# A deformable-convolution stage whose sampling window is six rows high instead of eight, with a separate stage for the samples that reach further

## The reference, cut to what matters

```
xr   = conv1x1(gn(x), w_reduce)            # 192 -> 180 channels
offs = conv1x1(xr, w_offset)               # 360 channels
off_w, off_h = offs[:, :180], offs[:, 180:]
# deform_conv2d, for each of 10 groups of 18 channels and each of 9 taps (ky, kx):
sy = off_y + (ky - 1) + h ;  sx = off_x + (kx - 1) + w
val = bilinear sample of xr at (sy, sx), zero outside the image
f_w, f_h = einsum('bikhw,oik->bohw', val, weight)     # 1620 x 180, one for each of two convolutions
attn = softmax(conv1x1(mean(f_w + f_h), w_attn))      # per image
out  = conv1x1(attn0 * f_h + attn1 * f_w, w_expand)
```

## Time and profile before

| | us |
|---|---|
| median of 3 runs | 13394.25 (13377.7 to 13395.6) |
| profiled execution, first to last instruction | 13389.0 |
| projections, from the first matmul of a chunk to the flag | about 82 to 474 |
| sampling and convolution, first DMA to last store | 474.9 to 8550 |
| all later stages | 8553 to 13389 |

### The profile page before, as it was taken

One profiled execution on the slowest core, in us unless ns is written; L12 is line 12 of the kernel. 1 busy time (PEld: TensorE's weight loads), 2 busy tenths in 40 slices (PEclk: granted clock), 3 DMA queues, 4 the chain that ended last, 5 costly groups with the idle time before them and its releaser, 6 DMA issues. The chain is left out here.

```text
span 13389.0 us, 237451 instructions
## 1 busy us (share of the span) xinstructions
PE 12626.2 (94%) x81086; PEld 10422.1 (78%) x81086; DVE 11629.7 (87%) x15744; ACT 11084.4 (83%) x13077; POOL 6971.2 (52%) x3614
## 2 busy tenths in 40 slices
PE   7899999999999999999999999988089989999999
PEld 4799999999999999999999999743053345555555
DVE  4699999999999999999999999778987878888888
ACT  2588888888888888888888888539777889899898
POOL 0255555555555555555555555303320068888887
PEclk9999999999999999999999999779599999999999
...
GB/s 122 162 178 177 178 178 178 178 178 178 178 178 178 178 177 178 178 178 177 177 178 178 177 178 178 189 149 153 136 173 143 156 111 104 99 106 104 100 104 85
DMA packets 824757, 2102.23 MB, mean 157 GB/s; under 512 B 83236, under 2 KB 430810, under 8 KB 681562
## 3 DMA queue, kind: packets, MB, share of 16 engines
...
## 5 line engine op out<-in xcount | busy, mean ns | idle before, releaser
L518 PE MATMUL dc_p<-dc_t 96*128 96x144 f32 x51948 | 6846.0, 285 | 21.1 <-PEq L515 20.8
L585 POOL TENSOR_TENSOR dc_t<-dc_t 128x648 f32<-128x648 f32 x2885 | 4526.4, 1569 | 4021.9 <-POOLq L584 3977.9
L518 PEld LDWEIGHTS dc_p<-dc_t 96*128 96x128 f32 x51948 | 6529.5, 189 | 42.4 <-issue 21.5
L645 DVE TENSOR_TENSOR dc_t<-dc_p,dc_t 128x1296 f32<-128x1296 f32 x2886 | 4342.9, 1505 | 507.3 <-DVEq L643 444.5
L464 ACT ACTIVATE dc_t<-dc_t 96x1152 f32<-96x1152 f32 x2892 | 3590.1, 1241 | 463.6 <-ACTq L488 462.3
L466 ACT ACTIVATE dc_t<-dc_t 96x1152 f32<-96x1152 f32 x2892 | 3367.8, 1165 | 347.5 <-ACTq L465 10.4
L2161 DVE TENSOR_TENSOR_SCAN ms_t<-ms_t,ms_p 128x512 f32<-128x512 f32 x1728 | 2127.7, 1271 | 282.8 <-PE ms_p L2103 204.6
L2077 POOL TENSOR_TENSOR ms_t<-ms_t 128x1536 f32<-128x1536 f32 x576 | 1987.8, 3456 | 503.5 <-DVE ms_t L2161 499.7
L2113 PE MATMUL ms_p<-ms_t,top_t 128*128 128x512 f32 x3456 | 1774.7, 596 | 0.0
L559 PE MATMUL dc_p<-dc_t 128*128 128x180 f32 (+1 forms) x7488 | 1633.5, 318 | 17.0 <-PEq L554 10.9
L2103 PEld LDWEIGHTS ms_p<-top_t,ms_t 128*128 128x128 f32 x6912 | 849.7, 141 | 967.6 <-issue 693.8
...
## 6 DMA issues: line engine op xcount, KB each, us to landing
dc_t<-sxd SPq DMA_DIRECT2D x1446, 864.0 KB, 5.7
ms_t<-bcd SPq DMA_DIRECT2D x576, 256.0 KB, 3.3
...
```

The costliest lines, as they stand in the source:

```text
L518: ins = e.matmul(PT[j % 2][:, t // 3, (t % 3) * 144:(t % 3 + 1) * 144], HX[:, m // 2 % RP, m % 2, t * 128:(t + 1) * 128], XW[:, i, ky:ky + ...
L585: e.tensor_tensor(z[:, :, 0:HALF], z[:, :, 0:HALF], z[:, :, HALF:2 * HALF], ALU.add)\
L645: e.tensor_tensor(Zt[:, n % 4, :].rearrange("p (b m i) -> p b m i", b=3, i=CG), PT[n % 2][:, :, 0:432].rearrange("p b (m i) -> p b m i", i ...
```

## The change

1. The sampling window is 6 rows instead of 8 (`WIN`), so the moving operand of a sample matmul is 108 columns instead of 144, `weigh` takes 972 columns instead of 1296, `halve` 486 instead of 648 (now into a tile of its own, `ZH`). Three rows remain: `quarter` adds the first two of them, `sum_rows` the third (324 columns each). `NWIN` is 17 instead of 13.
2. A window of 6 rows holds only samples whose vertical offset lies within `REACH` = 2.5 rows of its centre. In the projections stage the two reductions are replaced by the eight largest distances per partition and their indices (`max`, `max_index`), of an absolute value that ScalarE makes (`size`); SyncE also fills a DRAM array `cor` with zeros (96 DMAs of 270 KB).
3. A new stage `far_samples` collects up to 128 samples beyond reach, gathers their coordinates, the four `xr` vectors and the convolution weights by indirect DMAs from GpSimd, computes their contribution to the output, writes it to `cor` with an indirect DMA, and initialises `SUM` with it. It writes the flag: the loop over all windows is taken if there are more than 128 such samples, or more than 7 in a partition.
4. In sampling, each tile loads its part of `cor` and a factor (`kept_loads`), and GpSimd (`keep`) multiplies `ACC` by the factor and adds the correction, twice 128 x 360 once in a tile; VectorE's `scalar_tensor_tensor` in `add_up` becomes a `tensor_tensor`.
5. ScalarE makes hats for two steps in one instruction, 96 x 2304, and issues the Abs of the next pair ahead of the Relu of this one.
6. The tile store is issued by SyncE, in the row of its loads, instead of by ScalarE, one tile later than before.

```
-WIN = 8
-NWIN = 13
+WIN = 6
+NWIN = 17
-FAR = 3.0
+REACH = 2.5
+NCAND = 8
...
+                    for i in (2 * c, 2 * c + 1):
+                        e.dma_start(k.cor_z[i], Z[:, :, :].rearrange("p r c -> p (r c)")).then_inc(s_zs, 16)
...
+                    for u in range(3):
+                        ins = e.activation(AB[:, c % 3, u * CM:(u + 1) * CM], OY[:, c % 2, u, :], ACT.Abs,
+                                           bias=DT[:, u:u + 1])
...
+                def largest(c):
+                    e.wait_ge(s_ab, c + 1)
+                    e.max(k.CV[:, c, :], AB[:, c % 3, :]).then_inc(s_v, 1)
+                    e.wait_ge(s_v, 1).then_inc(s_v, -1)
+                    e.max_index(k.CI[:, c, :], k.CV[:, c, :], AB[:, c % 3, :]).then_inc(s_mx, 1)
...
-                    e.tensor_reduce(MM[:, 0, c:c + 1], OY[:, q, :, :], AX.XY, ALU.max)
-                    e.tensor_reduce(MM[:, 1, c:c + 1], OY[:, q, :, :], AX.XY, ALU.min).then_inc(s_o2, 1)
...
+                def kept_loads(i, b, ti, y):
+                    e.dma_start(CR[:, i, :], k.cor_v[DS(b * NT + y, 1)].rearrange("a p c -> (a p) c")).then_inc(s_cr[i % 2], 16)
+                    e.dma_start(KF[:, i:i + 1],
+                                k.d["c_keep"][DS(ti, 1)].rearrange("a p c -> (a p) c")).then_inc(s_cr[i % 2], 16)
...
+                            if q == 3:
+                                done = b * NT + y if i >= 2 else e.snap(((w + 15) >> 4) * NRB + (b * NT + y))
+                                store_tile(i, done, s_st[i % 2])
...
-                def hats(m):
-                    q, u = m // 2 % RP, m % 2
-                    if u == 0:
-                        e.wait_ge(s_bx[q], 16).then_inc(s_bx[q], -16)
-                    e.activation(HX[:, q, u, :], HX[:, q, u, :], ACT.Abs, bias=QX[:, 0:1]).then_inc(s_ab, 1)
+                def distance(q):
+                    e.wait_ge(s_bx[q % RP], 16).then_inc(s_bx[q % RP], -16)
+                    e.activation(HX[:, q % RP, :, :], HX[:, q % RP, :, :], ACT.Abs, bias=QX[:, 0:1]).then_inc(s_ab, 1)
+                def hats(q):
                     e.wait_ge(s_ab, 1).then_inc(s_ab, -1)
-                    e.activation(HX[:, q, u, :], HX[:, q, u, :], ACT.Relu, bias=1.0, scale=-1.0).then_inc(s_hx, 1)
+                    e.activation(HX[:, q % RP, :, :], HX[:, q % RP, :, :], ACT.Relu, bias=1.0, scale=-1.0)\
+                        .then_inc(s_hx, 2)
...
-                        if j == 3:
-                            y = y2 * NRB + i
-                            done = b * NT + y if i else e.snap(((w + 15) >> 4) * NRB + (b * NT + y))
-                            store_tile((i - 1) % NRB, done, s_st[(i - 1) % 2])
-                        hats((n + AHEAD) % NBB)
+                        if n % 2 == 0:
+                            distance((n + AHEAD) // 2 + 1)
+                            hats((n + AHEAD) // 2)
...
-                        ins = e.matmul(PT[j % 2][:, t // 3, (t % 3) * 144:(t % 3 + 1) * 144],
+                        ins = e.matmul(PT[j % 2][:, t // 3, (t % 3) * WIN * CG:(t % 3 + 1) * WIN * CG],
                                        HX[:, m // 2 % RP, m % 2, t * 128:(t + 1) * 128],
                                        XW[:, i, ky:ky + WIN, g * CG:(g + 1) * CG],
...
-                    e.tensor_tensor(z[:, :, 0:HALF], z[:, :, 0:HALF], z[:, :, HALF:2 * HALF], ALU.add)\
+                    e.tensor_tensor(ZH[:, n % 4, :, :], z[:, :, 0:HALF], z[:, :, HALF:2 * HALF], ALU.add)\
                         .then_inc(s_half, 1)
+                def keep(i):
+                    e.wait_ge(s_cr[i % 2], 32).then_inc(s_cr[i % 2], -32)
+                    e.tensor_scalar(ACC[:, i, :, :], ACC[:, i, :, :], KF[:, i:i + 1], None, ALU.mult).then_inc(s_pre, 1)
+                    e.wait_ge(s_pre, 1).then_inc(s_pre, -1)
+                    e.tensor_tensor(ACC[:, i, :, :], ACC[:, i, :, :], CR[:, i, :].rearrange("p (v c) -> p v c", v=2),
+                                    ALU.add).then_inc(s_acc, 1)
...
+                        if n % NB == 2:
+                            keep(n // NB)
...
-                e.memset(FT[:, :, :, :], 0.0).then_inc(s_out, 1)
+                e.memset(FT[:, :, :, :], 0.0).then_inc(s_out, 3)
...
-                    e.tensor_tensor(ZQ[:, n // 2 % 2, :, :], z[:, :, 0:2 * CG], z[:, :, 2 * CG:4 * CG], ALU.add)\
+                    e.tensor_tensor(ZQ[:, n // 2 % 2, :, :], z[:, :, 0:CG], z[:, :, CG:2 * CG], ALU.add)\
...
-                                    z[:, :, 0:CG], z[:, :, CG:2 * CG], ALU.add).then_inc(s_sum, 1)
+                                    ZQ[:, n // 2 % 2, :, :], z[:, :, 2 * CG:3 * CG], ALU.add).then_inc(s_sum, 1)
```

More of the change, by code:

```diff
@@ L8 @@
 I32 = mybir.dt.int32
+U32 = mybir.dt.uint32
 ACT = mybir.ActivationFunctionType
@@ L16 @@
 NT = HW // 128
-WIN = 8
-NWIN = 13
+WIN = 6
+NWIN = 17
 NCK = -(-NG * TAPS * CG // 128)
-FAR = 3.0
+REACH = 2.5
+NCAND = 8
+CPB = HW // 384
+NCH0 = B * CPB
 PADT = 4
-ROWS = 208
+ROWS = 108
 EPS = 1e-5
@@ L241, in _, with size @@
                 e.wait_ge(s_wr[0], 1).then_inc(s_wr[0], -1)
+                def size(c):
+                    e.wait_ge(s_oy, c + 1)
+                    if c >= 3:
+                        e.wait_ge(s_mx, c - 2)
+                    for u in range(3):
+                        ins = e.activation(AB[:, c % 3, u * CM:(u + 1) * CM], OY[:, c % 2, u, :], ACT.Abs,
+                                           bias=DT[:, u:u + 1])
+                    ins.then_inc(s_ab, 1)
                 norm(0)
@@ L249, in _ @@
                                      bias=BR[:, h:h + 1]).then_inc(s_xr, 1)
+                    if c >= 1:
+                        size(c - 1)
+                size(N - 1)
             @blk.tensor
@@ L294, in _ @@
                     offsets_x(c)
-                e.wait_ge(s_m, 1).then_inc(s_m, -1)
-                for i in range(2):
-                    ins = e.transpose(PT[0:1, 2 * i, 0:128], MX[:, i:i + 1], k.ident[:, :])
-                ins.then_inc(s_mt, 1)
             @blk.vector
@@ L380, in sample_and_convolve @@
         XW = p.sb([W, 2, WIN + 2, CM])
+        CR = p.sb([128, NRB, 2 * CM])
+        KF = p.sb([128, NRB])
         OYT = p.sb([128, 2, CM])
-        TAB = p.sb([128, NRB, WIN + 1])
+        TAB = p.sb([128, NRB, WIN])
         HX = p.sb([W, RP, 2, NPX])
@@ L452, in _ @@
                 e.wait_ge(s_free, RP + 2 - EXTRA).then_inc(s_free, EXTRA - 2 - RP)
+                store_tile(0, B * NT, s_fin)
+                store_tile(1, B * NT + 1, s_fin)
+                e.wait_ge(s_fin, 32).then_inc(s_fin, -32)
             @blk.scalar
@@ L482, in _ @@
                     row_weights(0, step)
-                for m in range(AHEAD):
-                    hats(m)
-                def store_tile(i, at, sem):
-                    e.wait_ge(s_out, 2).then_inc(s_out, -2)
-                    dst = k.d["fd"][DS(at, 1)].rearrange("y c (h p) x -> p (c h) (y x)", p=HM)
-                    e.dma_start(dst, FT[:, i % 2, :, :]).then_inc(sem, 16)
+                distance(0)
+                for q in range(AHEAD // 2):
+                    distance(q + 1)
+                    hats(q)
                 def body(b, y2, w):
@@ L618, in add_up @@
                     e.tensor_tensor(total, total, PF[:, conv * CM:(conv + 1) * CM], ALU.add)
+                    if conv == 0:
+                        e.wait_ge(s_acc, 1).then_inc(s_acc, -1)
                     a = ACC[:, i, conv, :]
-                    e.scalar_tensor_tensor(out=a, in0=a, scalar=TAB[:, i, WIN:WIN + 1],
-                                           in1=PF[:, conv * CM:(conv + 1) * CM], op0=ALU.mult, op1=ALU.add).then_inc(s_ff, 1)
+                    e.tensor_tensor(a, a, PF[:, conv * CM:(conv + 1) * CM], ALU.add).then_inc(s_ff, 1)
                 def keep_sum(i, conv):
@@ L2223, in program @@
             k.d[n] = nc.dram_tensor(n, shape, F32, kind=kind).ap()
+    k.xr_v = [k.d["xrT"][b * ROWS:b * ROWS + 208] for b in range(B)]
+    k.cor_z = k.d["cor"][0:B * HW * 2].rearrange("(i p r) c -> i p (r c)", p=W, r=4)
+    k.cor_v = k.d["cor"][0:B * HW * 2].rearrange("(t p v) c -> t p (v c)", p=128, v=2)
     k.oyd_v = k.d["oyd"].rearrange("b y x c -> b (y x) c").rearrange("b (t p) c -> b t p c", p=128)
@@ L2231, in program @@
         k.SUM = p.sb([128, B, 2, CM])
+        k.gathered = p.sems(4)
+        k.CV = p.sb([128, NCH0, NCAND])
+        k.CI = p.sb([128, NCH0, NCAND], U32)
         k.const_loads = [(k.ident[:, :], k.d["c_ident"]), (k.G6[:, :], k.d["c_g6"])]
@@ L2283, in layout @@
     w, r = np.arange(NWIN).reshape(1, NWIN, 1, 1), np.arange(WIN)
-    tab = np.zeros((2, NT, NWIN, 128, WIN + 1), f)
-    tab[0, ..., :WIN] = y - y0 + 3 - r
-    tab[1, ..., :WIN] = y - WIN * w + 1 - r
-    tab[1, :, 1:, :, WIN] = 1
-    d["c_tab"] = tab.reshape(-1, 128, WIN + 1)
+    tab = np.zeros((2, NT, NWIN, 128, WIN), f)
+    tab[0] = y - y0 + 2 - r
+    tab[1] = y - WIN * w + 1 - r
+    d["c_tab"] = tab.reshape(-1, 128, WIN)
+    keep = np.zeros((2, NT, NWIN, 128, 1), f)
```

(7 more changed lines are left out.)

327 lines of the change are left out of this document (277 added, 50 removed).

## The result

The changed kernel takes **12838.9 us** (median of 4, 12837.2 to 12854.5), the kernel before on the same chip 13386.0 us (4 runs, 13370.8 to 13395.6): a ratio of 0.9598 with a 95% interval of 0.9586 to 0.9610. The forecast was 12805, with 12640 to 13000 as its range. The profiled execution took 12837.9 us, its span is 12836.0 us. Two single executions in all that follows, one of e2 (28090.6 us) and one of e10 (18508.7 us), ran at a much lower mean granted clock (0.476 and 0.629) than the others and are left out of the ranges and intervals given.

What follows compares the result with a forecast made beforehand. TensorE was taken to set the sampling stage's pace, with the weight load the longer part at 108 columns. 13394 us, less 659 for narrower sample matmuls, plus 70 for the new stage, gave 12805 us, range 12640 to 13000.

Steps and rivals of the forecast that it cites:

- The pitch: Time between sample matmuls: from 122.6 ns to the 128-column weight load's 109.9 ns, scaled from a one-column row; bounds 108 to 112.
- The prediction's second way: Weight load of the sample matmuls from load durations: 189 - 81 = 108 ns for 127 more columns.
- The step: TensorE's sampling step: 18 matmuls gain 12.7 ns each, 2.786 to 2.557 us, 659 us gained over 2880 steps.
- The sum: Whole kernel: 13394 - 659 + 70 = 12805 us; 12800 for the profiled execution.
- VectorE and ScalarE: Sampling stage: neither bounds the step; VectorE 2.0 us a step, 79% of the stage, ScalarE 2.35 us, some 92%.
- single hats: ScalarE in sampling: hats left one step at a time would need 2.61 us a step and be the bound at 2.557.
- SyncE: Tile store and small loads in its queue cost nothing, hidden in slot waits of 551 of 610 us; store slack 10 us.
- Rival B: SyncE's store holds up the pair loads and TensorE stops once in a tile: 13960 us, chance 0.03.
- DMA: Sampling stage: the share of the engines' time goes from 0.70 to 0.76; pair loads stay hidden.
- Projections: Added maxima, ScalarE instructions and zero DMAs hidden behind TensorE; +2 us at the stage's end.
- The new stage: Between projections and sampling, alone on the path: +70 us, bounds 45 and 120, with 12 us of exposed DMA.
- Rival C: Sampling: load and matmul disturb each other or VectorE holds TensorE up; step 2.60 to 2.75 us, 12950 to 13370 us, chance 0.08.

Runs made afterwards that it cites:

- e2: Changed kernel with 144 instead of 108 moving columns in each sample matmul: 13395.7 us, ratio 1.0006.
- e10: Changed kernel with the new stage's tables loaded at program start, its strided sum as five whole sums, 140 small matmuls ahead of the first sample: 12834.4 us.
- e1: Changed kernel with 126 instead of 108 moving columns in each sample matmul: 12825.2 us.
- e8: Changed kernel with 72 moving columns in each sample matmul after four first tiles at 144, two window rows left out: 12840.2 us.
- e3: Changed kernel with 72 moving columns in each sample matmul from the third sample on, two window rows left out: 19639.8 us.
- e4: Changed kernel with ScalarE's hats made for one step at a time, as in the kernel before: 12828.1 us.
- e5: Kernel before with only the sample matmuls narrowed to 108 moving columns from the third sample on; other engines' work unchanged: 13134.3 us.
- e9: Changed kernel with the tile store issued by ScalarE again, at the third sample of the next tile: 12831.2 us.
- e6: Changed kernel without the new stage's work, SUM set to zero and the flag to one set of rows: 12786.0 us.

## Why the prediction was right, and where it was off

- **The pitch.** Forecast 109.9 ns within 108 and 112, measured 111.0. The step was the maximum of two pitches, and e1 and e8 show that this is how it works: 109 to 112 ns from 72 to 126 columns, 122.6 at 144. The one-column row of the mixing stage at a granted clock of 0.50, scaled by width and clock, came within 1%. The traces give the clock only as a share of full speed: the figures in GHz beside it in the prediction and the expectations are shown by none, and no term was worked out from them, the factor of 2 being 1.00 / 0.50. The scaling was lucky in part: by it 128 columns at 0.50 would be 154.5 x 128 / 90 = 219.7 ns, and e3 shows 213. The prediction's second way, 189 - 81 = 108 ns, which gave the lower bound, was luck: the 81 ns of L802 stand at a granted clock of 0.50, the 189 at 1.00, and against the 333 ns that a 128-column load lasts at 0.50 (e3) the difference is 252 ns, or 126 halved for a clock of 1.00.
- **The step.** 2.557 forecast, 2.573 measured; the missing 0.016 us is the pitch (18 x 1.1 ns = 0.020). Over 2880 steps 613 us and not 659: this is the one term that was mis-sized by more than 10 us, and 21 more went at the stage's start, where the sum had no term for a clock that has to rise again.
- **The sum.** For the profiled execution 12800 us were forecast and 12836 measured. The step gave 46 us too few, the stage's start took 21, the new stage cost 5 less than forecast; by these it would be 12862. The other 26 us, 18 in the projections and 8 behind sampling, had no term, and no run ties them to the change: that the sum came within 36 us is luck in this part.
- **VectorE and ScalarE.** 79% and 92% of the stage forecast, 79% and 85% measured. The claim that single hats would be the bound at 2.61 us was **wrong** (e4): I had taken the y-hats at the old 720 columns, 0.88 us, where the narrower tile makes them 540, 0.645 us (and 720 columns took 0.79 us in before, not 0.88); 2.43 + 4 x 0.645 / 20 is 2.56 us. Edit 5 does not keep the gain, it is worth nothing. That the cut in VectorE's columns is what keeps it was in the prediction as an unloading, "it comes to 2.0 us"; e5 gives the price, 0.12 us of a step or some 350 us, for VectorE's, GpSimd's and ScalarE's narrower work together.
- **SyncE.** Hidden, as forecast: 524 of 610 us of waits for slots, and e9 shows that the store costs nothing on either engine. Rival B did not occur, and from 1000 to 7800 us no wait of TensorE for hats appears.
- **DMA.** 0.76 forecast, 0.77 measured.
- **Projections.** Hidden, with 40.00 of 40 us on TensorE: `max` and `max_index` over 540 columns are 0.71 us each, so the bound of four reductions was not needed. The queues went from 0.37 to 0.66 with the zeros, and TensorE waited for nothing there.
- **The new stage.** +70 forecast, +65 measured, and e6 takes 53 away. The terms were near as well: exposed DMA was about 10 us where 12 were taken. The strided sum took 6.77 us where 1.05 ns a column would be 3.4. The data of the last gather were used 2.7 us after its issue began (501.07 to 503.81), and the four gathers were issued one after another 1.25 us apart; that is in the chain too.
- **Rival C**, a step of 2.60 to 2.75 us, is what e5 looks like. It did not occur in the changed kernel since VectorE has 1429 us of wait ahead of `weigh`.
